# A three-place ring for the key and query rows of plain attention, and a new order of its matmuls and moves

## The reference

```python
x = L0_attn_x                       # (8, 512, 256)
xn = _layernorm(x, axis=-1)
x = x + _L0_attn_ref(xn, ...) + _L0_ffn_ref(xn, ...)
...
q = (src @ Wq + bq).reshape(B, T, N_HEAD, HEAD_DIM)     # k, v likewise
scores = jnp.einsum('bqhd,bkhd->bhqk', q, k) * scale
probs = jax.nn.softmax(scores, axis=-1)
attn = jnp.einsum('bhqk,bkhd->bqhd', probs, v).reshape(B, T, D_MODEL)
attn = attn @ Wo + bo
x = _layer_norm(src + attn, ln1_g, ln1_b)
```

## Time and profile before

| what | value |
|---|---|
| median of 3 runs (lowest to highest) | 2158.83 us (2158.79 to 2159.38) |
| the profiled execution: its time, its span | 2159.92 us, 2158.1 us |
| PE busy in the span | 1818.1 us (84%), granted clock 0.916 of full |
| DVE, ACT, POOL busy | 1284.6, 834.5, 982.0 us |
| plain attention, first scores to last values | 62.5 to about 734 us |

### The profile page before, as it was taken

The page is one execution under the profiler, slowest core; times in us unless marked ns, Lnnn a source line. Parts: engine busy times, 40 slices in busy tenths (PEclk is TensorE's granted clock), DMA queues, the critical chain, the costliest instruction groups (busy, mean ns, idle before and its releaser), DMA issues.

```text
span 2158.1 us, 35151 instructions
## 1 busy us (share of the span) xinstructions
PE 1818.1 (84%) x11505; PEld 1072.7 (50%) x11506; DVE 1284.6 (60%) x2862; ACT 834.5 (39%) x1144; POOL 982.0 (46%) x624
## 2 busy tenths in 40 slices
PE   4877789789788603999948999999999999999998
PEld 1323334334233303999934464655546555564654
DVE  3564666666656442777766576665657656566661
ACT  1344355454444411444413425153342424425152
POOL 3212332323322553445443738557374763738454
PEclk8688899898889956999968999999999999999999
DMA  4553322412422253565440010000101001010000
GB/s 79 146 91 123 42 39 43 55 39 29 62 36 30 98 195 109 200 230 206 152 97 11 1 40 2 11 31 1 41 2 40 2 11 31 1 40 1 10 21 11
DMA packets 72147, 130.04 MB, mean 60 GB/s; under 512 B 11047, under 2 KB 50119, under 8 KB 66125
## 3 DMA queue, kind: packets, MB, share of 16 engines
q1 hardware_dynamic: 68940, 119.89, 21.5%
q0 software_dynamic: 3072, 8.39, 1.2%
HBM read 76.09 MB, written 26.74 MB: 48 GB/s over the span
## 4 chain that ended last, share of the span: by engine, by line
PE 36%; issue 7%; POOL 3%; DVE 3%; ACT 1%; POOLq 0%; DMA 0%; SPq 0%; DVEq 0%; ACTq 0%
PE a_psS L703 10%; PE a_psO L717 9%; PE a_psO L740 6%; PE a_psM L677 4%; PE a_psS L665 4%; PE a_psS L649 2%; POOL a_k_tok L350 1%; PE a_psS L730 1%; ACT a_probs L468 1%; POOL a_oT L373 1%; POOL a_q_tok L350 1%; DVE a_junk L534 1%; DVE a_alibi L611 0%; DVE a_qL L524 0%; DVE a_rden L548 0%
## 5 line engine op out<-in xcount | busy, mean ns | idle before, releaser
L385 POOL TENSOR_TENSOR a_probs<-a_probs 128x1024 f32<-128x1024 f32 x144 | 340.7, 2392 | 316.5 <-PE a_psO L717 316.5
L534 DVE CUSTOM_DVE_ANT_0 a_junk<-a_psM,a_alibi 128x512 bf16<-128x512 f32 x512 | 333.8, 689 | 216.1 <-PE a_psM L677 216.1
L1277 DVE TENSOR_REDUCE f_n_tok<-f_psR 128x1 f32<-128x512 f32 x512 | 325.0, 682 | 226.0 <-PE f_psR L1414 224.9
L468 ACT ACTIVATE a_probs<-a_psS 128x1024 f32<-128x1024 f32 x256 | 248.9, 1024 | 284.6 <-PE a_psS L703 284.5
L1223 ACT ACTIVATE f_probs<-f_psS 128x1024 f32<-128x1024 f32 x256 | 247.7, 1021 | 217.1 <-PE f_psS L1435 217.0
L1414 PE MATMUL f_psR<-f_kP,f_qP 48*128 48x512 f32 x512 | 177.1, 551 | 114.3 <-DMA f_qP<-f_low 75.8
L717 PE MATMUL a_psO<-a_probs,a_v 128*32 128x512 f32 x2048 | 244.0, 597 | 0.0
L1414 PEld LDWEIGHTS f_psR<-f_kP,f_qP 48*128 48x128 f32 x512 | 69.4, 206 | 306.2 <-DVE f_n_tok L1277 133.2
L1448 PE MATMUL f_psO<-f_probs,f_v 128*32 128x512 f32 x1024 | 155.4, 682 | 0.7 <-ACT f_probs L1223 0.6
L677 PE MATMUL a_psM<-a_kH,a_qH 64*128 64x512 f32 x512 | 125.4, 485 | 34.5 <-DVE a_n_tok L534 29.0
L740 PE MATMUL a_psO<-a_wo,a_oT 128*128 128x256 f32 x512 | 132.0, 406 | 4.4 <-POOL a_oT L373 4.4
(11 more groups left out here) (190 smaller groups left out, 3511.3 us busy)
## 6 DMA issues: line engine op xcount, KB each, us to landing
w_w_high<-w_parts SPq DMA_DIRECT2D x19, 1024.0 KB, 5.3
w_w_low<-w_parts SPq DMA_DIRECT2D x19, 1024.0 KB, 7.3
f_kP<-f_high SPq DMA_DIRECT2D x64, 128.0 KB, 4.6
f_qP<-f_high SPq DMA_DIRECT2D x64, 128.0 KB, 6.2
sorted_x<-f_zeros SPq DMA_DIRECT2D x1, 4864.0 KB, 21.7
e_xs<-sorted_x SPq DMA_DIRECT2D x19, 256.0 KB, 2.7
sorted_z<-e_z SPq DMA_DIRECT2D x19, 256.0 KB, 2.2
f_xn<-in_L_attn_x SPq DMA_DIRECT2D x8, 512.0 KB, 4.1
```

The lines of the kernel that those rows point to most:

```text
L385: nc.gpsimd.tensor_tensor(slots, slots, probs[:, first - GRP:first - GRP + 2, :], ALU.add).then_inc(added.sem, 1)
L468: nc.scalar.activation(probs[:, slots, :], psS[:, 2 * p:2 * p + 2, :], ACT.Exp).then_inc(exp_done.sem, 1)
L534: nc.vector.tensor_tensor_reduce(out=junk[:, a, :], in0=psM[:, a, :], in1=alibi[:, h, :], scale=1.0, scalar=-3.0e38, op0=ALU.add, op1=ALU.max,
L1277: nc.vector.tensor_reduce(n_tok[:, c, column:column + 1], psR[:, ring_bank("max", u), :], AX.X, ALU.max, negate=True).then_inc(max_done.se ...
```

## The change

`kP` and `qP` get 12 places instead of 8, three for each half of the pairs, used in turn (`place_of`). `move_sides(b + 1, g)` then waits for the scores that used its place three halves earlier. On SP, `move_sides(b + 1, 1)` goes from behind `move_maxima(b + 1, 0)` to between `move_maxima(b, 2)` and `move_maxima(b, 3)`, and `move_sides(b + 1, 0)` from behind `move_maxima(b, 2)` to ahead of it. On PE the late products go ahead of the values, and the transposes of the maxima leave `psS` for the ring `psR`. The clearing of `sorted_x` is cut into 8 DMAs, one for each batch, the W1 work is spread over the batches, the hardware loops are written out, and the start of the phase is reordered.

```diff
+    EXTRAS[0, 2] = [("maxima", 1)] + EXTRAS[0, 2]
+    TURNED = {(0, 3): [("rows", 0, 0), ("rows", 1, 2)]}
+    FILL = -(-(TILES * TOK // P) // B)
...
+    def place_of(b, pair):
+
+        return (2 * b + pair // HP) % 3 * HP + pair % HP
...
-        kP = sb("kP", [P, PAIRS, S], F32R)
-        qP = sb("qP", [P, PAIRS, S], F32R)
+        kP = sb("kP", [P, 3 * HP, S], F32R)
+        qP = sb("qP", [P, 3 * HP, S], F32R)
...
             def move_sides(b, g):
 
-                if not (isinstance(b, int) and b == 0):
-                    sp.wait_ge(score_ps.sem, score_ps.at(b - 1, QP * (2 * g + 2) * TT - 1))
-                    sp.sem_inc(passed, 1)
+                former = divmod(2 * b + g - 3, 2)
+                if former[0] >= 0:
+                    sp.wait_ge(score_ps.sem, score_ps.at(former[0], QP * (2 * former[1] + 2) * TT - 1))
...
             move_sides(0, 0)
             load_rows(0)
+            move_sides(0, 1)
             move_maxima(0, 0)
-            move_sides(0, 1)
-            sp.dma_start(sorted_x.rearrange("(n p) d -> p n d", p=P),
-                         zeros[:, :].unsqueeze(1).to_broadcast([P, TILES * TOK // P, D])).then_inc(cleared, 16)
...
-            def batch(b, more, last):
+            for b in range(B):
+                more = b + 1 < B
                 move_maxima(b, 1)
+                if b + 2 < B:
+                    load_rows(b + 1)
+                if more:
+                    move_sides(b + 1, 0)
                 move_maxima(b, 2)
                 if more:
-                    if not last:
-                        load_rows(b + 1)
-                    move_sides(b + 1, 0)
+                    move_sides(b + 1, 1)
                 move_maxima(b, 3)
+                if b % 2 == 0:
+                    if b:
+                        store_w1(b // 2 - 1)
+                    load_w1(b // 2)
+                clear_rows(b)
                 if more:
                     move_maxima(b + 1, 0)
-                    move_sides(b + 1, 1)
...
             nc.gpsimd.memset(wo[:, :, :], 0.0).then_inc(zeroed, 1)
+            nc.gpsimd.memset(zeros[:, :], 0.0).then_inc(zeroed, 1)
+            nc.gpsimd.memset(v[:, :, :, FH:], 1.0).then_inc(zeroed, 1)
+            norm0.raise_variance(pool, 0)
             nc.gpsimd.memset(kP[:, :, :].bitcast(F32), 1.0).then_inc(zeroed, 1)
             nc.gpsimd.memset(qP[:, :, :].bitcast(F32), 0.0).then_inc(zeroed, 1)
-            norm0.raise_variance(pool, 0)
-            nc.gpsimd.memset(zeros[:, :], 0.0).then_inc(zeroed, 1)
-            nc.gpsimd.memset(v[:, :, :, FH:], 1.0).then_inc(zeroed, 1)
...
-            batch(0, False, True, range(NE // 2))
-            with pool.Fori(1, B - 1) as b:
-                batch(b, True, True)
-            batch(B - 1, True, False, range(NE // 2, NE))
+                if b % 2:
+                    split_w1(b // 2)
+
+            for b in range(B):
+                batch(b, b > 0, b + 1 < B)
...
                     for p in range(QP):
                         scores(b, r, p, before)
+                    for u in late:
+                        if present(b, "max", u):
+                            multiply_for_max(b, u)
                     if r:
                         weigh(b, r - 1)
                     elif before:
                         weigh(b - 1, PERIODS - 1)
-                    for u in late:
-                        if present(b, "max", u):
-                            multiply_for_max(b, u)
...
+            pe.wait_ge(zeroed, ZEROED)
+            for u in range(AHEAD - 4):
                 multiply_for_max(-1, u)
-            pe.wait_ge(xnT_sb.sem, xnT_sb.at(0, 0))
-            transpose(-1, "maxima", 0, 0)
+            turn_maxima(-1, 0)
+            for u in range(AHEAD - 4, AHEAD):
+                multiply_for_max(-1, u)
```

More of the change, by code:

```diff
@@ L1140, in _, with batch @@
             keep_rows(0, True)
-            def batch(b, before, more, splits=()):
+            def batch(b, before, more):
                 if more:
@@ L1153, in batch @@
                     low_part(b + 1, 1)
-                for e in splits[0:1]:
-                    split_w1(e)
                 normalize(b, 1)
@@ L1230, in batch @@
                         exponentials(b, r, p)
-                    for kind, n, bank in turned_in(b, r):
-                        take(b, kind, n, bank, not before and n == 1)
+                    for kind, c, bank in turned_in(b, r):
+                        take_rows(b + 1, c, bank)
                     if j == 0:
@@ L1239, in batch @@
                             take_output(b - 1, QUADS - 1)
-                    if more:
-                        for kind, n in EXTRAS.get((quad, j), ()):
-                            if kind == "proj":
-                                take_sides(b + 1, n)
+                    for kind, n in EXTRAS.get((quad, j), ()):
+                        if kind == "proj" and more:
+                            take_sides(b + 1, n)
+                        elif kind == "maxima" and present(b, kind, n):
+                            take_maxima(b + belongs(kind, n), n)
             for c in range(KC):
-                take(-1, "rows", c, 2 * c)
+                take_rows(0, c, 2 * c)
+            act.wait_ge(loads, LOADS)
+            nc.scalar.mul(bqk[:, 1::2], bqk[:, 1::2], FH ** -0.5).then_inc(scaled, 1)
+            act.wait_ge(scaled, SCALED + 1)
             for n in range(SIDES):
                 take_sides(0, n, True)
-            take(-1, "maxima", 0, 0, True)
-            batch(0, False, True)
-            with act.Fori(1, B - 1) as b:
-                batch(b, True, True)
-            batch(B - 1, True, False)
+            take_maxima(0, 0)
+            for b in range(B):
+                batch(b, b > 0, b + 1 < B)
             take_output(B - 1, QUADS - 1)
```

142 lines of the change are left out of this document (59 added, 83 removed).

## The result

The changed kernel took 2178.53 us (median of 6 runs, 2169.91 to 2197.48), the kernel before 2158.81 us beside it (median of 6, 2148.97 to 2160.63). The ratio is 1.0108, with a 95% interval of 1.0064 to 1.0153: **slower by about 1.1%**. I had predicted 2138 us. The profiled execution took 2177.51 us, its span is 2175.7 us, and the granted clock is 0.913.

The account below looks back on a forecast made before the run. PE's queue, standing still at r = 10 and r = 2, was taken to pace plain attention's batches. Terms +1 - 10.2 - 12.6 + 8 - 7 = -20.8 us took 2159.9 to 2139.1, as median 2138 us; range 2122 to 2154.

Parts of the forecast that it names:

- The start, +1: Start of the first phase: POOL's memsets hold DVE's normalising operations, so PE's transposes start at 19.6, not 18.69: +1 us.
- The small DMAs queue behind the moves: Plain attention, r = 8 and r = 12: maxima's DMAs wait behind 12 moves, 14.9 us from first move to scores.
- The rival that they don't: Plain attention: small DMAs don't queue, no wait at r = 8, a batch 9.5 us shorter, 2071 us; chance 0.08.
- the rival that only the wait at r = 8 vanishes: Plain attention: half 0's k and q moves go out with a gap, -3.9 x 7, 2111 us; chance 0.09.
- Scores of r = 8: Plain attention batch: they come 22.3 us behind the scores of r = 4, against 18.6 before: +3.7 us.
- r = 12 to the next batch: End of a plain attention batch: slow start, inversion, transposes and v projection take 16.3 us against 19.5: -3.2.
- r = 0 to 4, predicted 22.8: Start of a plain attention batch: 25.4 us less the 2.6 wait and 0.8 for transposes, plus 0.8 for DVE: 22.8.
- Batches 2 to 6, +8 in all: Plain attention: a new batch takes 85.8 us against a mean of 84.2, +1.6 x 5 = +8 us.
- Batch 0, -10.2: First batch of plain attention: without big clearing and W1 load on the queue, 88.7 us becomes 78.5: -10.2 us.
- Batch 1, -12.6: Plain attention: W1 loaded and split earlier, batch 1 becomes an ordinary one, 98.4 us to 85.8: -12.6 us.
- Batch 7, -7: Last plain attention batch: loses its wait at r = 2 and the slow clock behind, 66.4 to 59.4: -7 us.
- The rival "slower: the clock": Plain attention: PE's two long stands lower its clock four periods more behind both, 10 us a batch, 2211 us; chance 0.11.

Follow-up runs that it names:

- act_queue: Changed kernel with the small DMAs of the maxima issued by ACT on its own queue, not SP's: 2117.29 us, ratio 0.981.
- late_back: Changed kernel with the two late products for maxima behind the values again: 2200.96 us, ratio 1.022.
- pad_after_8: Changed kernel with 8 idle semaphore additions more on PE at the start of the routing phase: 2179.11 us, ratio 1.0111.
- pad_before_96: Kernel before with 96 idle semaphore additions more on PE at the start of the routing phase: 2181.27 us, ratio 1.0128.
- pad_before: Kernel before with 156 idle semaphore additions more on PE at the start of the rotary phase: 2162.88 us, ratio 1.003.
- pad_after: Changed kernel with 100 idle semaphore additions more on PE at the start of the rotary phase: 2152.48 us, ratio 0.9964.
- queue_pad: act_queue with 32 idle semaphore additions more on PE at the start of the routing phase: 2092.92 us, ratio 0.9707.
- queue_pad_r3: queue_pad with only the two late products of r = 3 behind the values again: 2076.97 us, ratio 0.9642.
- queue_pad_r13: queue_pad_r3 with the late products of r = 1 behind the values as well: 2066.6 us, ratio 0.959.
- sp_order: Changed kernel with 32 idle PE instructions and, on SP, `move_maxima(b, 3)` ahead of `move_sides(b + 1, 1)`: 2102.03 us, ratio 0.9747.
- two_places: queue_pad without the third place, so each pair has one place again: 2113.31 us, ratio 0.9811.

## Why the prediction was wrong

The sign was wrong: 2138 predicted, with 0.11 for slower, and 2178.5 measured, outside the range. Against the two profiled executions, the difference of 17.6 us of span is -9.0 in plain attention and +26.6 in the rotary phase. My sum was -20.8 for the first and had no term for the second.

**The step that failed** is the second sentence: "Only the first phase changes, so I look for what ends last there." The source of the rotary phase is the same, but its place in PE's program is not. Writing out the loops raised PE's instructions ahead of it, and by the place of the stop the loop's top came to lie some 24 instructions ahead of a fetch boundary. The fourteen traces fall into two groups. Where a stall named issue stands at line 703 (changed kernel, its repeat, act_queue, late_back, pad_after_8, pad_before_96) rotary takes 903.9 to 908.2 us. Where it does not (kernel before, pad_before, pad_after, queue_pad, queue_pad_r3, queue_pad_r13, sp_order, two_places) it takes 870.9 to 881.1 us. Idle instructions alone moved the kernel before into the slow group and the changed one out of it, and each stall ends 1.2 to 1.6 us behind the landing of a fetch packet. The stalls account for 13.8 of the 26.6 us; the slow clock behind them, which the windows show, is a further part. How the rest divides no run separates.

Point by point in plain attention:

- *The start, +1*: 62.5 to 63.5. DVE's normalisation of the first rows ended at 7.97 + 11.41 = 19.38 us, predicted "near 19.5". The first of the four operations lasted from 7.97 to 18.42, under POOL's two memsets (7.91 to 13.12 and 13.06 to 18.27), so DVE did not get in between them:

```profile
7.97 11.41 DVE L115 TENSOR_SCALAR f_xn<-f_xn,f_norm_aggr,f_norm_rstd 128x256 f32<-128x256 f32 x4 [1.16 <-POOL f_norm_rstd L82]
```

- *The small DMAs queue behind the moves*: right, at both places, but not in size at r = 8. The waits at r = 12 are 9.6 to 11.0 us in batches 0 to 6 (8 to 11 predicted), those at r = 8 only 1.5 to 2.8 (3 to 5 predicted), in three of the seven below 2 us, the first half of a sign of being wrong that I had named (the second half, under 6 us at r = 12, did not come). That the total came to 90 all the same is partly luck: r = 12 stood at the upper end. The rival that they don't had 0.08; the rival that only the wait at r = 8 vanishes fell as well. sp_order and act_queue show the cause by removing it in two ways.
- *Scores of r = 8*: from r = 4 it is 368.52 - 347.25 = 21.3 us in batch 3 (22.3 predicted). The first move went out at 354.50, as predicted 7.2 us behind r = 4. But the scores came 14.0 us later, not 14.9, and without their wait of 1.64 it would have been 19.6 us, not 18.3.
- *r = 12 to the next batch*: 16.3 us in batch 3, as predicted. r = 8 takes 2.2 us, not 3.3.
- *r = 0 to 4, predicted 22.8*: 26.1 us in batch 3 and 27.7 in batch 4. This is the mis-sized term. r = 3 alone went from 7.0 us before to 10.1. I credited late products ahead of the values as feeding DVE and took the wait at r = 2 for gone. I did not name what stands behind a late product that waits: at r = 3 the values and an output projection, at r = 1 the values and a v projection. In queue_pad_r13, with both moved back, r = 0 to 4 takes 22.8 and 23.5 us in batches 3 and 4 (2.23 + 5.95 + 6.99 + 7.62 in the first); in queue_pad, which differs from it only by these products, it is 26.1 and 27.8.
- *Batches 2 to 6, +8 in all*: 87.4 us against the predicted 85.8, so +15.8. Batch 1 with 89.3 us is over the 89 that I had named as another sign of being wrong.
- *Batch 0, -10.2*: 88.7 to 81.8, so -6.9. *Batch 1, -12.6*: 98.4 to 89.3, so -9.1. Both gains show, 3.3 and 3.5 us smaller than I said. In batch 1 it is the term above, r = 0 to 4 with 27.7 us; batch 0 I had only worked out as a whole.
- *Batch 7, -7*: 93.7 us to POOL's last addition became 83.9, so -9.8. To the end of the last values, near which my 66.4 us ended, it is -9.0 (63.6 to 54.6).
- *The rival "slower: the clock"*: the result has its sign, but not by its mechanism. Behind the stand at r = 12 the values are slow (1.93 us) in one or two periods, as behind the stand at r = 10 of the kernel before. The clock did matter where I had not priced it, at r = 3 and behind the rotary stalls.

The sum by measured terms is +1.0 - 6.9 - 9.1 + 15.8 - 9.8 = -9.0. So even in its own phase the change won less than half of what I said. The waits for the maxima, which I had priced rightly in sum and taken as given, were the larger part of what there was to win: act_queue took 61 us from the changed kernel.

## What to carry to other kernels

An edit that changes how many instructions one engine has can slow a hardware loop far behind it: compare the phases that you did not touch, look for waits named issue at a fixed instruction behind a loop's top, see whether the stop ends just behind a packet of the instruction queue, and shift the loop by a few instructions in a place where the engine waits anyway. A small DMA on which the next matmul depends should not stand on a queue behind bulk moves that have periods of slack; move the call or give it another engine's queue. Before a matmul is put ahead of others, ask for each period what it could wait for and what then stands behind it, and count the slow clock behind every stop with the stop.

## What the runs showed of the hardware

- A loop of PE whose top lies shortly ahead of a boundary of the instruction fetch stops there once per turn, for 1.5 to 4.1 us, and lost some 24 us in six turns (903.9 against 878.7 us for the kernel before with and without 96 idle instructions). A shift of 8 instructions moves the stop by four matmuls (each counts as two), a shift of 32 removes it. The Trainium skill (Runtime: NRT & Kernel Launch, Instruction fetch mechanics) calls a boundary mostly hidden. The trace agrees for the rest of the loop, where behind the first product no other wait named issue of a microsecond stands, and not for a boundary so close behind the jump to the top. The stop varies between 1.5 and 4.1 us with the landing of its packet, 1.2 to 1.6 us before PE goes on. Why some packets come late no run shows; transfers are under way there (DMA share 0.52 in the window above).
- Not every loop of PE is fetched anew. In the kernel before no packet of q8 starts between 240.8 and 692.6 us, while PE runs its loop over the batches of plain attention (819 recorded instructions in batch 2); the rotary loop (1844 recorded) brings 8 to 10 packets in each turn. Where the limit lies between the two no run shows.
- My count of PE's instructions gave the one distance that can be read right (8 instructions, four matmuls) and fits 32, 96 and 100, but it did not give the boundary itself from one program to the other: pad_before missed by it.
- 100 to 156 additions to a semaphore cost PE about 0.04 us each (3.9 and 6.7 us) where nothing hides them.
- Turns without the stall come in two lengths, about 129.5 and 127.8 us, also within one run (queue_pad_r3, pad_before). r = 3 and r = 1 of plain attention have two lengths as well (10.1 and 8.4, 7.8 and 6.15). Both stay open.
